# A decoder's sorted-expert stage: stores behind loads, a third row buffer, squares on ScalarE, sums in place

## The reference

```python
# layer 0; ln is a layer norm without weights
x = x + attention(ln(x))               # 16 heads of 64, relative position bias, softmax over 1024
x = x + cross_attention(ln(x), ctx)    # 8 heads, 64 context rows in 4 windows
h = bfloat16(ln(x))                    # mixture of experts: 8 experts, 2 per token
n = bfloat16(h * rsqrt(mean(h * h) + eps) * norm_weight)
s, e = top_k(bfloat16(n @ gate.T + gate_bias), 2)
w = softmax(s)
g, l = split(n @ w1[e].T + b1[e])      # even and odd columns
p = min(g, 7) * sigmoid(1.702 * min(g, 7)) * (clip(l, -7, 7) + 1)
x = x + (h + bfloat16(sum over both of w * (p @ w2[e].T + b2[e])))
# layer 1
x = x + groups(ln(x))                  # attention and feed-forward in groups of 32, local, then strided
x = x + rotary_cross_attention(ln(x), ctx)
x = x + low_rank_mixture(ln(x))
```

## Time and profile before

| | |
|---|---|
| median of three runs | 2193.9 us |
| profiled execution: its time, its span | 2199.73 us, 2197.9 us |
| TensorE busy, weight loads busy | 1906.6 us (87%), 1579.2 us (72%) |
| VectorE, ScalarE, GpSimd busy | 1303.5, 971.4, 966.4 us |
| mean granted TensorE clock | 0.93 |

### The profile page before, as it was taken

One profiled execution on the slowest core, in us unless ns is written; L12 is line 12 of the kernel. 1 busy time (PEld: TensorE's weight loads), 2 busy tenths in 40 slices (PEclk: granted clock), 3 DMA queues, 4 the chain that ended last, 5 costly groups with the idle time before them and its releaser, 6 DMA issues.

```text
span 2197.9 us, 52542 instructions
## 1 busy us (share of the span) xinstructions
PE 1906.6 (87%) x21476; PEld 1579.2 (72%) x21476; DVE 1303.5 (59%) x2964; ACT 971.4 (44%) x1952; POOL 966.4 (44%) x783
## 2 busy tenths in 40 slices
PE   7999999999999999666355528999999999998994
PEld 5677777777777777455244427999989999987883
DVE  6767676667677666267522336555556545555883
ACT  3666666666666665311222203424334423424551
POOL 2555555555555555245311162334334334344441
PEclk9999999999999999898566658999999999999996
DMA  7001020102311001342211142000022010031000
GB/s 261 16 18 56 11 80 11 56 28 112 119 38 49 11 11 39 123 144 73 74 46 44 55 144 84 12 21 13 12 85 73 17 31 17 17 119 28 11 16 15
DMA packets 75149, 120.37 MB, mean 55 GB/s; under 512 B 8424, under 2 KB 65008, under 8 KB 71536
## 3 DMA queue, kind: packets, MB, share of 16 engines
q1 hardware_dynamic: 69504, 102.68, 14.0%
q0 software_dynamic: 2560, 6.30, 1.0%
q10 hardware_dynamic: 2848, 8.04, 1.0%
HBM read 77.14 MB, written 39.85 MB: 53 GB/s over the span
## 4 chain that ended last, share of the span: by engine, by line
PE 40%; DMA 5%; DVE 5%; issue 4%; POOL 2%; SPq 2%; ACT 2%; POOLq 0%; DVEq 0%; ACTq 0%
PE psum L265 12%; PE psum L276 8%; PE psum L1999 4%; PE psum L1987 2%; DMA b_xs<-xs 2%; PE psum L2491 2%; PE psum L225 2%; PE psum L1333 2%; PE psum L1973 2%; PE psum L2525 1%; PE psum L1350 1%; PE psum L1243 1%; DMA b_x_in<-in_x 1%; PE psum L246 1%; ACT e_pr L2630 1%
## 5 line engine op out<-in xcount | busy, mean ns | idle before, releaser
L770 POOL TENSOR_TENSOR a_sm<-a_sm,a_rsum 128x1024 f32<-128x1024 f32 x256 | 479.9, 1894 | 356.7 <-DVE a_rsum L804 354.3
L792 DVE CUSTOM_DVE_ANT_0 a_sm<-psum,a_strip 128x1024 f32<-128x1024 f32 x256 | 312.0, 1219 | 146.6 <-PE psum L624 146.6
L705 ACT ACTIVATE a_sm<-a_sm,a_mn 128x1024 f32<-128x1024 f32 x256 | 293.9, 1148 | 28.2 <-DVE a_mn L792 26.9
L637 PE MATMUL psum<-ident,a_sm 128*128 128x128 f32 x2048 | 275.2, 277 | 5.2 <-POOL a_sm L770 4.2
L710 ACT ACTIVATE a_pT<-psum 128x512 f32<-128x512 f32 x256 | 151.6, 592 | 273.0 <-PE psum L637 273.0
L637 PEld LDWEIGHTS psum<-ident,a_sm 128*128 128x128 f32 x2048 | 223.8, 140 | 62.7 <-issue 46.0
L652 PE MATMUL psum<-a_pT,a_V 128*64 128x256 f32 x2048 | 249.0, 385 | 0.6 <-ACT a_o L716 0.6
L652 PEld LDWEIGHTS psum<-a_pT,a_V 128*64 128x64 f32 x2048 | 136.1, 136 | 77.3 <-issue 22.1
L799 DVE COPY a_pT<-psum 128x512 f32<-128x512 f32 x256 | 174.9, 683 | 12.2 <-PE psum L637 4.9
L2083 ACT ACTIVATE g_val<-psum 128x512 f32<-128x512 f32 x64 | 38.1, 597 | 217.7 <-PE psum L1999 217.7
L624 PE MATMUL psum<-a_KH,a_QH 64*128 64x512 f32 x512 | 114.7, 445 | 2.5 <-DVE a_mn L792 2.5
(11 more groups left out here) (393 smaller groups left out, 3946.5 us busy)
## 6 DMA issues: line engine op xcount, KB each, us to landing
a_strip<-table SPq DMA_DIRECT2D x16, 960.0 KB, 6.8
oT<-a_o SPq DMA_DIRECT2D x64, 128.0 KB, 1.9
xs<-b_zeros SPq DMA_DIRECT2D x8, 1024.0 KB, 4.1
b_oT_in<-oT SPq DMA_DIRECT2D x8, 1024.0 KB, 6.4
y<-b_yb SPq DMA_DIRECT2D x23, 256.0 KB, 2.1
b_xs<-xs SPq DMA_DIRECT2D x23, 128.0 KB, 2.2
a_raw<-in_a_wqkv SPq DMA_DIRECT2D x7, 384.0 KB, 3.3
s_x<-in_x_rev SPq DMA_DIRECT2D x4, 512.0 KB, 7.4
```

Of the source, the lines that this page charges most:

```text
L637: last = pe.transpose(psum[:, 4 + j, k * P:(k + 1) * P], sm[:, st % RING, kt * P:(kt + 1) * P], ident[:, :])
L705: a.activation(sm[:, st % RING, :], sm[:, st % RING, :], ACT.Exp, scale=-1.0, bias=mn[:, at:at + 1], accum_out=rsum[:, at:at + 1]).then_in ...
L770: g.tensor_tensor(sm[:, st % RING, :], sm[:, st % RING, :], rsum[:, at:at + 1].broadcast_to([P, T]), ALU.mult).then_inc(sig("scaled"), 1)
L792: v.tensor_tensor_reduce(out=sm[:, st % RING, :], in0=scores_banks(hl).rearrange("p c n -> p (c n)"), in1=strip[:, pair % 2, hl, qt * P:qt ...
```

## The change

- SP's expert loop stores the result of tile j-2 behind the fetch of tile j+3, where it stored that of tile j.
- A third row buffer (`b_oT_in2`, `b_x_in2`) lies over the expert stage's `xs`, `xT` and part of `yb`. `fetch(s)` waits for `ay_out` s-2, `fetch(2)` for nothing. The buffers' semaphores are `lx0` to `lx2`, which the expert stage's fetches count on from.
- The expert weights are loaded by SP, behind the rows of tiles 1 and 2 and the context of tile 2; only the bias `b1` is asked for before them. ScalarE widens `w2` in its round 4 and fills `pick` in round 5. The query weights of the groups are asked for behind all row loads.
- The squares are done on ScalarE (`Square` with an accumulator) at the end of its round.
- `combined` writes tiles 0 and 1 straight into the groups' `g_x`. The reload is gone; the groups' first norm stands behind `combined(0)`, its root behind gather 1.
- GpSimd's `first_sum(1)` stands behind its constants.

```diff
     def sync(sp, then):
         def fetch(s):
             tok = slice(s * CP, (s + 1) * CP)
-            sp.wait_ge(sig("ay_out"), s - 1)
-            oT, x, _, _ = slots[s % 2]
+            if s > 2:
+                sp.wait_ge(sig("ay_out"), s - 2)
+            oT, x = slots[s % 3][:2]
...
         def store(s):
             r = s % 2
+            rows = then["rows"][:, s, :, :] if s < 2 else x3[:, r, :, :]
...
         load_rows(sp, have, 1, mixture_rows(A, S, slots, 1))
+        load_weights(sp, have, weights[:1])
+        fetch(2)
         fetch_context(2)
-        for s in range(2, NP):
+        load_weights(sp, have, weights[1:])
+        for s in range(3, NP):
             fetch(s)
-            if s + 1 < NP:
-                fetch_context(s + 1)
-            if s == 4:
-                sp.wait_ge(sig("wide"), 2)
-                then["load_queries"](sp)
+            if s > 3:
+                fetch_context(s - 1)
+        fetch_context(NP - 1)
+        sp.wait_ge(sig("wide"), 2)
+        then["load_queries"](sp)
...
-        for j in range(NU):
+        for j in range(NU + 2):
             if j + UR < NU:
                 fetch_sorted(j + UR)
-            store_sorted(j)
+            if j >= 2:
+                store_sorted(j - 2)
         for s in range(NP):
             store(s)
-            if s == 1:
-                for r in range(2):
-                    sp.wait_ge(sig(f"st{r}"), 16 * (1 + P // SEG))
-                then["load_first"](sp)
...
     def scalar(a, then):
-        load_weights(a, have, weights)
...
-            if r == 0:
+            if r == 4:
+                a.wait_ge(have("w2b"), 16)
                 a.activation(w2[:, :, :, :], w2b[:, :, :, :], ACT.Copy).then_inc(sig("wide"), 1)
-            if r == 1:
+            if r == 5:
...
+            if 0 <= b < NP:
+                for t in range(PT):
+                    a.wait_ge(sig("mn_h"), PT * b + t + 1)
+                    if b:
+                        a.wait_ge(sig("m_normed"), PT * b)
+                    a.activation(junk[:, t, :], xc[:, b, t, :], ACT.Square, accum_out=ss[:, t:t + 1]).then_inc(sig("m_ss"), 1)
...
         for s in range(NP):
             gather(s)
-            if s == 3:
+            if s == 1:
                 then["first_root"](g)
...
         def squares(s):
             norm_apply(v, sig, "mn", s, x2[:, s, :, :], xc[:, s, :, :], mn)
-            for t in range(PT):
-                v.wait_ge(sig("mn_h"), PT * s + t + 1)
-                if s:
-                    v.wait_ge(sig("m_normed"), PT * s)
-                v.scalar_tensor_tensor(junk[:, t, :], xc[:, s, t, :], 1.0, xc[:, s, t, :], ALU.mult, ALU.mult,
-                                       accum_out=ss[:, t:t + 1]).then_inc(sig("m_ss"), 1)
...
-            if s >= 2:
+            if s >= 4:
                 v.wait_ge(sig(f"st{r}"), 16 * (1 + P // SEG) * (s // 2))
-            v.tensor_tensor(x3[:, r, :, :], x2[:, s, :, :], mo[:, :, :], ALU.add).then_inc(sig("x3"), 1)
-
-        v.wait_ge(have("w2b"), 16 * 2)
+            rows = then["rows"][:, s, :, :] if s < 2 else x3[:, r, :, :]
+            v.tensor_tensor(rows, x2[:, s, :, :], mo[:, :, :], ALU.add).then_inc(sig("x3"), 1)
+
+        v.wait_ge(have("b1"), 16)
...
-        for s in range(3):
-            combined(s)
+        combined(0)
         then["first_stats"](v)
+        combined(1)
+        then["first_norm"](v)
+        combined(2)
+        then["low_columns"](v)
         combined(3)
-        then["first_norm"](v)
         combined(4)
-        then["low_columns"](v)
         combined(5)
         then["first_keys"](v, (0, 1))
...
     def loaded(eng, s):
         if s < 2:
-            eng.wait_ge(have(f"rows{s}"), 16)
+            eng.wait_ge(before["signals"][0]("x3"), s + 1)
```

More of the change, by code:

```diff
@@ L1055, in cross_and_mixture @@
     sig, have = early["sig"], early["have"]
-    have.reserve("rows1 w1 w2b")
+    have.reserve("rows1 w1 w2b b1")
     routed = Signals(nc, "r")
     routed.reserve("sc gy0 gy1")
-    sig.reserve("made mc_out br_out br_ps by_out by_ps filled ld0 ld1 lw0 lw1 lw2 lx0 lx1 lx2 m2_out m2_ps mT_out mT_ps "
+    sig.reserve("made mc_out br_out br_ps by_out by_ps filled lw0 lw1 lw2 lx0 lx1 lx2 m2_out m2_ps mT_out mT_ps "
                 "m_act m_exp m_gap m_hi m_lo m_mask m_normed m_out m_rms m_seen m_spot m_ss mc_ps mg_out mg_ps "
@@ L1170, in loaded_context @@
             eng.wait_ge(sig(f"lw{s % 3}"), 16 * 2 * ((s - 2) // 3 + 1))
-    weights = [("w2b", w2b[:, :, :, :], A["m_w2"]), ("w2b", b1b[:, :, :, :], A["m_b1"]),
+    weights = [("b1", b1b[:, :, :, :], A["m_b1"]), ("w2b", w2b[:, :, :, :], A["m_w2"]),
                ("w1", w1[:, :, :, :].rearrange("p k e n -> p k (e n)"), A["m_w1"])]
@@ L1190, in store @@
             r = s % 2
+            rows = then["rows"][:, s, :, :] if s < 2 else x3[:, r, :, :]
             sp.wait_ge(sig("x3"), s + 1)
             sp.dma_start(S["x3"][s * CP:(s + 1) * CP, :].rearrange("(t p) d -> p t d", p=P),
-                         x3[:, r, :, :]).then_inc(sig(f"st{r}"), 16)
+                         rows).then_inc(sig(f"st{r}"), 16)
             grid = S["x3p"].rearrange("(b i s t l) d -> b s l i t d", b=B, i=SEG, s=BP, t=PT)
@@ L1196, in store @@
                 sp.dma_start(grid[s // BP, s % BP, l, :, :, :],
-                             x3[l * SEG:(l + 1) * SEG, r, :, :]).then_inc(sig(f"st{r}"), 16)
+                             rows[l * SEG:(l + 1) * SEG, :, :]).then_inc(sig(f"st{r}"), 16)
         def fetch_sorted(j):
@@ L1242, in attended @@
             for k in range(HP):
-                last = pe.matmul(bank[:, t * D:(t + 1) * D], slots[s % 2][0][:, k, t * P:(t + 1) * P], wo[:, k, :],
+                last = pe.matmul(bank[:, t * D:(t + 1) * D], slots[s % 3][0][:, k, t * P:(t + 1) * P], wo[:, k, :],
                                  start=k == 0, stop=k == HP - 1)
@@ L1442, in first_sum @@
             loaded(g, s)
-            g.tensor_tensor(slots[s % 2][1][:, :, :], slots[s % 2][1][:, :, :], over_tiles(bo_a[:, :], PT), ALU.add).then_inc(sig("x_bo"), 1)
+            g.tensor_tensor(slots[s % 3][1][:, :, :], slots[s % 3][1][:, :, :], over_tiles(bo_a[:, :], PT), ALU.add).then_inc(sig("x_bo"), 1)
         def scatter(s):
@@ L1480, in gpsimd @@
                         channel_multiplier=0).then_inc(sig("filled"), 1)
+        first_sum(1)
         for signals in old:
@@ L1554, in joined @@
                 v.wait_ge(sig("by_out"), s - 1)
-            v.tensor_tensor(x1[s % 2][:, :, :], tiles_of(banks("ay", s)), slots[s % 2][1][:, :, :], ALU.add).then_inc(sig("ay_out"), 1)
+            v.tensor_tensor(x1[s % 2][:, :, :], tiles_of(banks("ay", s)), slots[s % 3][1][:, :, :], ALU.add).then_inc(sig("ay_out"), 1)
             v.wait_ge(sig("ay_out"), s + 1)
@@ L1770, in group_attentions @@
                 "ld_e1 ld_res0 ld_res1 ld_x0 ld_x1 result st v_chain w_hi w_lo")
-    have.reserve("b1 pw rows0 rows1 vec w1 w2 wk wq wv")
+    have.reserve("b1 pw vec w1 w2 wk wq wv")
     room, where = before["where"], {}
@@ L1864, in loaded @@
             eng.wait_ge(sig(f"ld_e{s % 2}"), 16 * ((s - NP) // 2 + 1))
-    def load_first(sp):
-        for s in range(2):
-            load_rows(sp, have, s, [rows_in(s)])
     def load_queries(sp):
@@ L2350, in vector @@
         then["steps_vector"](v, last_sum, last_norm)
-    return {"load_first": load_first, "load_queries": load_queries, "load_projections": load_projections, "load_rest": load_rest, "first_units": first_units,
+    return {"rows": x, "load_queries": load_queries, "load_projections": load_projections, "load_rest": load_rest, "first_units": first_units,
             "high_part": lambda a, i: high_part(a, 0, i), "first_columns": lambda a: high_columns(a, 0),
```

17 lines of the change are left out of this document (9 added, 8 removed).

## The result

The changed kernel takes 2054.13 us (median of 4 runs, 2049.87 to 2061.38), the kernel before beside it 2196.44 (4 runs, 2191.62 to 2201.97): ratio 0.9355, interval 0.9318 to 0.9391, 142 us less. Forecast were 2049 us, 2034 to 2088. A second measurement on another chip gave 2061.88 against 2198.43, ratio 0.9388 (0.9368 to 0.9408), 137 us less. The profiled execution of the changed kernel is the fastest of its runs (2049.87, span 2048.1), and the trace of before is of one above its median, so the two traces are 149.8 us apart: 25.8 in the rounds, 107.6 from the first fetch to the last store, 12.9 in the combining stage, 4.6 behind it, less 1.2 by which the first row load of the stage starts later.

What follows compares the result with a forecast made beforehand. The expert stage was taken as bound by a circle of waits: each row fetch stood behind the store of TensorE's latest result. Gains of 112, 19 and 14 us, 145 in all, from 2193.9 gave 2049 us, range 2034 to 2088.

Steps and rivals of the forecast that it cites:

- the rounds: Rounds before the expert stage: all their edits together gain 19 us, between 3 and 24.
- Stores behind two loads: Expert stage: the transfer leaves the path, which then binds only below some 2.1 us a turn; gain 112 us.
- The turn: Expert loop: one turn takes 2.8 us, between 2.6 and 4.7, with about 2.5 us of TensorE work.
- The start: Expert stage: the first fetch behind two projection weights still takes 6.31 us, so turn 0 begins at 1083.3.
- Clock: Expert stage: without the stall TensorE's granted clock stays above 0.9; 1.3 us added for a low first turn.
- Rival 1: Expert stage: the clock stays low, turns take 4.7 us, the stage gains 75 us, time 2086; chance 0.1.
- Entry: Entry of the rounds: tile 1's rows load without the expert weights, TensorE starts 7 us sooner; bounds 0 and 9.
- Third buffer: Rounds: rows asked for a full round earlier, TensorE's row-buffer waits shrink; gain 7 us, bounds 3 and 9.
- Squares: Rounds: moving squares off VectorE, which sets the round, gains 5 us; bounds 3 lost and 6 gained.
- The 3 us lost: Rounds: by the skill's rule, squares on ScalarE would lose about 0.4 us a round, 3 us.
- `w2` and `pick`: Rounds 4 and 5: filling them in ScalarE's idle gap costs nothing, up to 1 us each if it closes.
- Sums in place: Combining stage: no reload and an earlier norm of tile 0, keys ready for VectorE; gain 14 us, bounds 4 and 16.

Runs made afterwards that it cites:

- e1: The kernel before with one edit, result stores placed behind two row loads in the expert stage: 2092.21 us, ratio 0.9530.
- e5: The changed kernel with every sorted tile sent through expert 0, so no expert is picked by register: 2060.25 us, ratio 0.9358.
- e8: The changed kernel with the expert weights asked for at the entry of the rounds on ScalarE's queue, as before: 2072.28 us, ratio 0.9410.
- e9: The changed kernel with each row load of the rounds waiting one residual longer, as with two buffers: 2059.83 us, ratio 0.9372.
- the seven: Seven profiles of kernels whose rounds are the changed kernel's: rounds of 141.8 to 148.8 us, mean 145.7.
- e2: The changed kernel with the result stores put back ahead of the fetches, as in the kernel before: 2162.62 us, ratio 0.9836.
- e10: The changed kernel with tile 0's statistics, norm, columns and root moved later again, sums still written in place: 2065.41 us, ratio 0.9398.
- e4: The changed kernel with the two squares of a tile back on VectorE: 2060.01 us, ratio 0.9373.
- e12: The changed kernel itself, unchanged, measured again on another chip: 2061.88 us, ratio 0.9388.
- e7: The changed kernel with a round's two output biases added by TensorE in PSUM in place of GpSimd's sums: 2052.01 us, ratio 0.9322.

## Why the prediction was right

The time (2049 for 2054) and the main cause, a circle through the result store, were right; of its terms two were not. That the sum came so near is in part luck: by the runs, the stores were taken 5 us too high and the sums in place 7.5, the rounds 5 too low.

- *Stores behind two loads*, 112 us: from turn 0 to the landing of the last store 179.0 us became 70.0, 109 us (107.6 from the first fetch), and e1 shows it alone with 106.3. The turn is 3.0 us, not 2.8, which over 20 turns is 4 us: the matmuls were sized right (2.51 in e5) and the register work before them was missing. The start I had as unchanged, 6.31 us, is 7.69. The path binds at 2.5 us a turn already, not only below 2.1.
- *Clock*, taken as high: TensorE's granted clock is 1.00 from 1070 to 1120. The Trainium skill (TensorE: Matmul & The Clock Gate, "Loop structure matters more than you think") has matmuls warm beside running transfers; the trace agrees. Rival 1 is out: with four transposes in each turn, matmuls ran at the high clock throughout.
- *Entry*, 7 us: 7.5 between the first two traces (14.4 and 6.9 us from the first row load to the projection), 8.0 in e8. Right.
- *Third buffer*, 7 us: the waits for `x_in` went, as said, but the buffer was not why (e9). This step failed in its cause: I read "TensorE waits for the row buffer" as too few buffers and didn't look at what SP had queued ahead of the load. It was also too small. By the mean of the seven the rounds are 24.3 us shorter than the mean of e1 and before, 170 us; against e2 and e10, which have three caught operations as these two have, it is 21. Less 8 and 4.5, some 9 to 12 us are left for the rows' place in the queue.
- *Squares*, 5 us: 4.5 in e4. The 3 us lost that the prediction worked out by the Trainium skill's rule (ScalarE: Activation LUTs, "Rules for kernel authors") are not borne out. `w2` and `pick` aren't in the chain of the changed kernel's first trace; in e12 `w2` stands in it with 3.60 us, and in e7, with the biases gone from GpSimd, `pick` does. No run takes them out alone.
- *Sums in place*, 14 us: 6.5. The state after was sized right: the forecast had the statistics at 1311.6, 48.6 us after the first gather, and they stand at 49.6, with the last gather issued at 43.1 (46.8 before). The step that failed is the state before. I charged all of VectorE's 10.27 us ahead of the first key copy to the order of the norm, but in that trace the 96 matmuls of queries and keys took 19.7 us; in e1, with the same order and no gaps, they take 13 and the stage 56.0 in place of 62.5. The two first traces agreed with 14 by accident.

With the measured sizes the sum is 107 + 24 + 6.5, some 137 us. e12 is 137 below before as well, but by other parts: 4.4 in the combining stage and 2.0 behind it. The first 142 is within what the combining stage and the rounds scatter.

## What to carry to other kernels

When a queue serves both loads and stores, ask for each load what stands ahead of it and when that is released, before counting buffers: here the expert stage was bound by it (a store, shown by e1 and e2), and by all signs the rounds too (the load of keys and values, argued), and both cures were a reordering. Once the wait is gone the loop runs at the engine's own pace, and that pace is the matmuls plus the register work between them. Size a term by two traces only where the rest of the code runs alike in both, and look first for single instructions that take far longer than their like: their number explained the scatter of the rounds.

## What the hardware did that was not expected

- A VectorE operation of 0.16 us took 3.16 us and ended with GpSimd's second sum. The Trainium skill (SBUF — State Buffer, "Who interferes with whom") says that the two engines share a port pair under an exclusive lock, held for a whole instruction. The trace agrees, and e7, without the sums, has no such operation. It shows more: the wait ran over two sums in a row and part of a descriptor job.
- TensorE's instructions can come late: single matmuls up to 2.8 us apart, start to start, while GpSimd issues gathers and for 3 to 4 us after the last, in all eight traces from two chips, in none of four from a third, and in the trace of before. In the kernels with the changed order the stage was 5 to 9 us longer with it. What delays them was not tried.
- Matmuls whose weights are picked by a register start 0.124 to 0.134 us apart in the changed kernel, the same without it (e5) 0.109; in a turn, 0.5 us.
